# Weight chunks behind the fetched result rows, the overflow count before step 0, and 14 filler matmuls for 20, in a two-layer graph and expert kernel

## What is computed

```
x = x + L0_gnn(layernorm(x), edges)        # adjacency, three diffusion steps, relu
x = x + L0_ffn(layernorm(x))               # 8 experts, two chosen per token
x = x + L1_gnn(layernorm(x), edges, attr)  # messages, sums per node, a GRU cell, batch norm
x = x + L1_ffn(layernorm(x))               # 8 LSTM experts, two chosen per token

L0_ffn: logits = relu(x @ gw1 + gb1) @ gw2 + gb2; the two largest, softmaxed, weigh
        gelu(x @ we1[e] + be1[e]) @ we2[e] + be2[e]
L1_gnn: m = relu([h[src], attr] @ W1.T + b1) @ W2.T + b2; agg = segment_sum(m, dst)
        gi = agg @ W_ih.T + b_ih; gh = h @ W_hh.T + b_hh; gates r, z, n of a GRU
```

## Time and profile before

| | us |
|---|---|
| three runs | 482.66, 488.34, 490.34 |
| their median | 488.34 |
| the profiled execution | 483.48 |
| its span, from the first to the last instruction | 481.7 |

### The profile page before, as it was taken

The page is one execution under the profiler, slowest core; times in us unless marked ns, Lnnn a source line. Parts: engine busy times, 40 slices in busy tenths (PEclk is TensorE's granted clock), DMA queues, the critical chain, the costliest instruction groups (busy, mean ns, idle before and its releaser), DMA issues.

```text
span 481.7 us, 6148 instructions
## 1 busy us (share of the span) xinstructions
PE 439.2 (91%) x2214; PEld 351.2 (73%) x2214; DVE 396.8 (82%) x645; ACT 281.5 (58%) x306; POOL 106.6 (22%) x128
## 2 busy tenths in 40 slices
PE   3988799999999976899999998979899899999895
PEld 1655578788888766587899996647678788887674
DVE  8989868898889854687999979785898998978764
ACT  2245468768876744143444446254988788858631
POOL 5641000111100050146787300030001211000300
PEclk9999999999999997799999999988999999999897
DMA  7931557899998838378677333235688999975801
GB/s 256 304 124 44 190 199 270 303 353 358 377 361 320 340 105 366 105 267 312 190 208 260 97 109 140 103 135 174 246 306 322 348 373 363 363 299 215 353 2 45
DMA packets 25780, 115.67 MB, mean 240 GB/s; under 512 B 7036, under 2 KB 7708, under 8 KB 14864
## 3 DMA queue, kind: packets, MB, share of 16 engines
q1 hardware_dynamic: 18400, 93.90, 52.7%
q0 software_dynamic: 7056, 21.26, 13.4%
q10 hardware_dynamic: 288, 0.03, 0.1%
HBM read 108.63 MB, written 6.55 MB: 239 GB/s over the span
## 4 chain that ended last, share of the span: by engine, by line
PE 63%; DVE 21%; ACT 6%; DMA 5%; issue 3%; POOL 1%; DVEq 1%; ACTq 0%; SPq 0%; POOLq 0%
PE bank L1506 11%; PE bank L1507 11%; PE bank L1511 11%; DVE wlo L928 7%; PE bank L1499 4%; PE bank L1882 3%; PE bank L1500 3%; PE bank L1884 3%; PE bank L1501 3%; PE bank L1520 2%; DMA y_tok<-y_rows,row_i 2%; PE bank L1771 2%; PE bank L1709 2%; DMA raw<-in_weights_dram 1%; ACT whi L673 1%
## 5 line engine op out<-in xcount | busy, mean ns | idle before, releaser
L928 DVE TENSOR_TENSOR wlo<-raw,whi 128x2048 fp32r<-128x2048 f32 x73 | 165.2, 2287 | 15.0 <-ACT whi L673 14.5
L673 ACT ACTIVATE whi<-raw 128x2048 fp32r<-128x2048 f32 x73 | 137.6, 1914 | 8.3 <-PE bank L1851 6.4
L1506 PE MATMUL bank<-whi,xe_hi 128*128 128x512 f32 x192 | 77.2, 402 | 2.8 <-ACT xe_hi L702 1.4
L1507 PE MATMUL bank<-wlo,xe_hi 128*128 128x512 f32 x192 | 75.9, 395 | 0.0
L1511 PE MATMUL bank<-whi,xe_lo 128*128 128x512 f32 x192 | 52.4, 394 | 0.0
L1506 PE MATMUL bank<-whi,hT_hi 128*128 128x512 f32 (+1 forms) x124 | 49.8, 405 | 2.1 <-ACT hT_hi L730 1.4
L615 POOL DMA_INDIRECT xg<-node_rows,idx x12 | 14.4, 1202 | 156.9 <-DVE idx L1191 156.9
L1507 PE MATMUL bank<-wlo,hT_hi 128*128 128x512 f32 (+1 forms) x124 | 48.1, 391 | 0.0
L648 POOL DMA_INDIRECT gath<-node_rows,src_i x34 | 41.6, 1224 | 15.2 <-DVE mp L1423 8.7
L1506 PEld LDWEIGHTS bank<-whi,xe_hi 128*128 128x128 f32 x192 | 36.1, 188 | 11.6 <-issue 2.2
L1511 PEld LDWEIGHTS bank<-whi,xe_lo 128*128 128x128 f32 x192 | 36.1, 188 | 8.6
(11 more groups left out here) (307 smaller groups left out, 854.2 us busy)
## 6 DMA issues: line engine op xcount, KB each, us to landing
raw<-in_weights_dram SPq DMA_DIRECT2D x85, 1024.0 KB, 6.3
y_rows<-y_sb POOLq DMA_DIRECT2D x16, 256.0 KB, 5.9
ea<-in_ea_dram SPq DMA_DIRECT2D x8, 256.0 KB
node_rows<-xn POOLq DMA_DIRECT2D x4, 256.0 KB, 2.5
gath<-node_rows,src_i POOLq DMA_INDIRECT x34
x<-in_x_dram SPq DMA_DIRECT2D x1, 512.0 KB, 3.8
gw<-in_L_ffn_gw_dram SPq DMA_DIRECT2D x1, 512.0 KB, 10.2
node_rows<-A_sb POOLq DMA_DIRECT2D x2, 256.0 KB, 4.4
```

The lines of the kernel that those rows point to most:

```text
L673: act.activation(whi[n % SPL][:, :, :], raw[n % RAW][:, :, :], ACT.Copy).then_inc(hi_cut, 1)
L928: dve.tensor_tensor(wlo[n % SPL][:, :, :], raw[n % RAW][:, :, :], whi[n % SPL][:, :, :].bitcast(f32), ALU.subtract).then_inc(lo_cut, 1)
L1506: pe.matmul(ps, xh[:, blocks + k, :], whi[w % SPL][:, k, cs], start=first and k == 0, stop=False)
L1507: pe.matmul(ps, xh[:, blocks + k, :], wlo[w % SPL][:, k, cs], start=False, stop=False)
```

## The change

Three edits. SP issues only W1's chunk ahead and waits for the four result fetches of layer 0 (`y_in`) before the three Whh chunks. VectorE counts the overflow jobs and loads the register before step 0, right behind the selectors of expert 3, in both layers. The fillers between the layers are 14.

```diff
@@ sync
             main(FFN_ORDER[RAW - 1:])
             more(ffn)
-            main(GNN_ORDER[0:4])
+            main(GNN_ORDER[0:1])
+            sp.wait_ge(y_in, 16 * 2 * NT)
+            main(GNN_ORDER[1:4])
             sp.wait_ge(layer_done, 2)
@@ vector, experts(run)
                 build_g(3)
+                more_experts(run.layer + 1)
+                number = dve.value_load(more_i[run.layer][0:1, 0:1], min_val=0, max_val=MORE)
                 for step in range(E):
...
                     if step == 1:
                         expert_weights(run.layer + 1)
-                    elif step == 2:
-                        more_experts(run.layer + 1)
-                        number = dve.value_load(more_i[run.layer][0:1, 0:1], min_val=0, max_val=MORE)
                     elif step == 3:
@@ tensor
-            keep_busy(B[2], 20)
+            keep_busy(B[2], 14)
             pe.wait_ge(layer_done, 2)
             turn_x(2)
```

## The result

| | before | after |
|---|---|---|
| median, us | 487.76 (4 runs, 482.66 to 490.34) | 481.19 (4 runs, 481.03 to 481.92) |
| profiled execution, us | 483.48 | 481.92 |
| its span | 481.7 | 480.1 |
| mean granted clock | 0.969 | 0.955 |

The ratio is 0.9891 with an interval of [0.9844, 0.9938]: the medians are 6.6 us apart (1.3%), and the ratio, which goes by fast executions alone, makes it 5.3 us. The forecast was 478.6, or 7.3 us less. The two profiled executions differ by 1.6 us only; why that is so little is the second half of the reading.

What follows compares the result with a forecast made beforehand. The chain was 63% TensorE, with the result fetch setting the end of layer 0's experts. Terms -6.4 (layer end) + 0.6 (layer 0) - 1.5 (layer 1) = -7.3 us, from 485.9 to 478.6; range 472.5 to 486.5.

Steps and rivals of the forecast that it cites:

- Rival B: Overflow count stays on the path: 1.5 us lost in layer 0, stall at 95.49 stays, layer 1 nothing; 481.0, chance 0.12.
- Rival C: Clock falls in the gap behind the 14 fillers; W1 and Whh products take 2.5 us more; 481.1 us, chance 0.08.
- Part 1: End of layer 0's experts: three chunks behind the rows, landing at 183.8 for 189.15, last sums 4.8 us earlier.
- the middle bound: Result rows landing 6.2 us after the last issue, at 185.7, as in the middle of twelve fetches; 3.5 us saved.
- any landing before 184.3 is worth the same: End of layer 0's experts: with rows that early, TensorE's product and ScalarE's copy at 189.61 set the end.
- Rival A: Rows land as late as before, held by W1's chunk and the fetch's issue; -1.9 us, 484.0, chance 0.14.
- Part 2: Between the layers: 14 fillers at full clock take 3.0 us; 6.4 us saved with part 1, 1.0 us alone.
- Part 3, layer 1: Overflow count moved into VectorE's 3.34 us of idle time costs nothing and removes TensorE's 1.46 us index stall: -1.5 us.
- Part 3, layer 0: Overflow count before step 0: 1.5 us lost at expert 2's index, 0.9 won at a weight cut; net 0.6 lost.
- Gain at 95: Layer 0: TensorE's 0.89 us stall for a weight cut at 95.49 goes when the count leaves step 2; 0.9 us won.
- Loss at the index: Layer 0: expert 2's index comes at 67.7, so TensorE's turn of the activations, at 66.23, is 1.5 us later.
- Rival D: Slower: low clock at four places where TensorE idles, 2.5 us each, 2.7 us lost in all; 488.6, chance 0.04.

Runs made afterwards that it cites:

- the early chunks: Changed kernel with W1 and the first Whh chunk issued during the overflow job's cuts, the other two Whh chunks behind the result rows; 483.9 us, ratio 0.9944.
- the last run: Kernel with layer 0's count in steps 4 and 5 and fillers at its experts' begin, plus 8 and 5 fillers before layer 0's last sums; 475.72 us.
- the kernel with 20 fillers: Changed kernel with 20 fillers again between the layers in place of 14; 481.6 us, ratio 0.9894.
- late count: Changed kernel with layer 0's overflow count in step 4 and its register load in step 5, layer 1's still before step 0; 477.92 us, ratio 0.9806.

## Why the prediction was right, and where not

The total was close (481.2 for 478.6; -6.6 for -7.3) and inside the range. How near it came is in part luck: the terms that the traces show add up to less (below), and the measured 481.2 is nearer to what rivals B (481.0) and C (481.1) would have given. The time can't part these three; the traces do. Of the three terms layer 1's held, the layer end's was 1.9 us too large, and layer 0's loss had the right sign and under half the size.

**Part 1, the rows: right mechanism, one size off.** "I take 183.8" was 4.3 us behind the last issue; it took 6.18, at 185.7 on the old scale, which is the middle bound of the same paragraph, and the gain of the last sums was 16.17 - 13.06 = 3.1 us, near what it said for that bound (3.5), in place of 4.8. The failing step is "this one has the end of one, so I take 183.8, nearer to the sum of bytes". The traffic was over 1.6 us before the rows were reported. The landings, all from the last issue: 8.9 to 9.6 us with four chunks beside the fetches (three kernels), 6.1 to 6.2 with one (six kernels), 5.0 or 5.1 with one (the three kernels with fillers at the begin of the experts), 3.7 with none (two kernels). Why the same one chunk gave 5.0 and 6.2 stays open. Hence "any landing before 184.3 is worth the same" was not reached in the changed kernel; with the early chunks it was, and there VectorE waited 0.42 us for `y_hi` and ScalarE 2.70 us for the product. Rival A, rows as late as before, fell.

SP's queue behind the wait was as costed. The prediction named a wait of ScalarE for a Whh chunk as a sign of being wrong; there was one (0.93 us, at 192.41), but it ends before the transposed tile is there and costs nothing.

**Part 2, the fillers: nearly the forecast gain, with the clock wrong.** "I expect the full clock" failed. The step behind it, "TensorE stands still only from about 189.7 to 190.3 before the last sums", was wrong: the rows came later, and it stood 1.89 us in the changed kernel, 3.22 and 1.88 in others. So the 14 fillers took 4.72 us in place of 3.0, but ended almost when the tile was ready: tile at 197.78 + 0.58 = 198.4, transposes at 198.8. From the last sums to the transposes it was 6.70 us before and is 5.27 now: 1.4 us for the forecast 1.6. Together the end gave 4.5 for 6.4, 1.7 of the difference from the rows and 0.2 from the fillers. Rival C was right on the level in the fillers and wrong on the price: the last run had the full clock there and gained 1.0 us at the place, nothing in the time, and in the graph part's first products the clock was at 1.00 (198 to 200), where C had it low.

**Part 3, layer 1: right.** -1.6 us for the forecast -1.5, the block in VectorE's idle time.

**Part 3, layer 0: the index right, the fetch wrong.** Gain at 95: 1.1 us between the two profiles (forecast 0.9), 0.4 to 1.1 over all. Loss at the index: the turn waited 1.79 us in place of 0.57, so 1.2 us late (forecast 1.5; the block took 3.7 us there, 63.25 to 66.91, and not 4.0). The failing step is "a fetch of 3.4 us is there by 72, one of the middle 6.2 us 1 to 2 us late; nothing else loads the queues much there, so I take the first and cost it at nothing". The rows were late by 1.3 us (step 1 took 14.76 us for 13.51), 7.7 us behind the issue and not 3.4. Two things were missing: POOL's issue grew to 3.1 us beside VectorE's cuts, and two weight chunks, issued at 70.10, did load the queues. Net of layer 0: 1.2 + 1.3 - 1.1 = 1.4 us lost for 0.6. In the four profiles with the moved count where the clock stayed low until 64 or later, the changed kernel's own among them, both losses are hidden behind TensorE's slower work. With layer 1's -1.6 the third edit comes to about nothing, and its run alone, and the one that leaves it out, show no gain either. Moving layer 0's block to steps 4 and 5 brought 3.3 us by medians of different sets (481.19 to 477.92); the terms would give 2.5. Rival B, that the block moves on the path, was true of layer 0's index, but the stall at 95 did shrink, and it was false of layer 1.

The terms that the traces show come to -4.5 + 1.4 - 1.6 = -4.7 us; the ratio says -5.3 (interval -7.6 to -3.0), the medians -6.6. What the last 0.6 to 1.9 us are stays open: the wait and the fillers alone gave -3.3 and -0.8 by ratio, both together -5.2, each with some 2 us of uncertainty. Rival D, slower through the clock at four places, fell with the ratio. Its price can be read at one of them: layer 1's step 1, behind the wait of 1.94 us, takes 13.27 us in three profiles (before among them) and 14.5 to 14.6 in the other eleven; the granted clock there was 1.00 before and 0.51 in 339.1 to 341.1 in the changed kernel. That is 1.3 us a fall, not 2.5. Two of the eleven lack the count's move, so the fall needs no edit; but of the ten profiles with the count moved in layer 1 only one kept the clock, of the four without it two, and whether the edit makes it more frequent stays open.

## What to carry to other kernels

Where a layer's end waits for small fetches, put the big loads behind them, but keep the one load that the next engine's queue needs first: both extremes here were worse than the middle. Before moving work in front of an index, look at what the late index's DMA issue will then run beside and which bulk loads will be in the queues ahead of it, not only at who waits for the index. Compare two profiles stretch by stretch at shared instructions before believing their spans: a clock that fell in one of them, ahead of the edits, took 3.4 us of the difference here.

## What the hardware did that was not expected

**POOL's issue of an indirect DMA beside VectorE.** 1.06 us with no weight cut beside it, 3.10 and 3.11 us when VectorE had begun a 128x2048 subtraction of two operands 0.12 to 0.14 us before. The Trainium skill, "SBUF — State Buffer", section "Terms", says that VectorE and GpSimd arbitrate for a shared pair of ports that is held for a full instruction, so that the loser blocks. The rows agree: the extra 2.04 us is about what was left of the first of the two cuts (2.29 - 0.14 = 2.15), and the issue ends 0.95 us behind that cut's end, about as long as an issue takes with nothing beside it. So do the first two result fetches in the kernel before, 1.72 and 1.90 us long, which end 0.9 us behind the ends of the two overflow cuts at 172.61. That the ports are what is held, no run here shows. An issue begun ahead of a cut got through in one case (0.97 us at 394.94, the cut at 395.14) and not in another (3.49 us at 382.09, the cut at 382.46).

**The register load.** The Trainium skill, "DMA: Bandwidth & Descriptors", section "Latency and other measured facts", gives about 600 ns as its floor. Behind the block VectorE stood still 1.65 us (layer 0) and 1.03 us (layer 1) before, and 1.30 us in the new place, with no releaser shown. All three lie above that floor. The prediction said that the trace disagrees with the page; it doesn't, it only shows that the floor is not what the load cost here.

**Fetches' tails.** In 186 to 188 the DMA engines moved 12 GB/s, and the rows were reported at 187.65: at least 1.6 us in which almost nothing moved and VectorE was not yet released.

**The clock, execution by execution.** Layer 0's begin took 21.3 us in five of the fourteen profiles, 22.6 to 22.8 in four (two of them by the late index, two by a fall of the clock that was over by 62) and 24.1 to 25.3 in five. One of those five, the kernel with 20 fillers, has both the late index and the fall. Six profiles have layer 0's count ahead of step 0 and the old fillers at the begin: the clock fell in five of them, and not in that of the early chunks. Of the five with the old fillers and the count elsewhere it fell in two. The fall starts ten microseconds ahead of the count, so no row makes the count its cause, and whether it is, stays open. Over all timed executions of each set the mean granted clock was 0.967 for the kernel before in the first set, 0.962 with the count alone, 0.971 without it or with it late, 0.978 with fillers at layer 0's begin, 0.983 with those before the last sums too. The time follows it only in part: from 0.971 (late count) to 0.978 it fell by 2.0 us, from there to 0.983, in another set, by 0.2.
